# Layer 3 of a four-layer program: another order of three engines' instruction lists

## The chip, the cores and the metric

One core of one Trainium2 chip. A core has TensorE (PE), VectorE (DVE), ScalarE (ACT), GpSimd (POOL) and SyncE (SP, which only issues DMAs here). Each works through its own list of instructions in order, and they wait for each other by semaphores. The metric is the device time of the whole program in microseconds, lower is better; a change under 0.2% can't be told from none.

## What is computed

A residual stream x of 16 batches of 256 tokens, 128 wide, goes through four layers, each of the form below. The change touches layer 3 alone.

```python
xn = _layernorm(x, axis=-1)
x = x + _L3_attn_ref(xn, ...) + _L3_ffn_ref(xn, ...)

# _L3_attn_ref: a state space scan over time, 16 states for each of 128 channels
delta = softplus(x @ W_delta.T);  B = x @ W_B.T;  C = x @ W_C.T;  A = -exp(A_log)
h = h * exp(delta_t * A) + (delta_t * x_t) * B_t;   y_t = sum_n h * C_t
context = (_layer_norm(y) @ W_ctx.T) * context_scale

# _L3_ffn_ref: 8 routed experts (top 2 by router logits, softmax gates) and 2 shared ones
expert(xf) = silu(xf @ w1) * (xf @ w3) @ w2
```

## The kernel before

The program is built by Python generators. A generator holds what one engine does for one batch in one stage, and each `yield` parts it into steps. In layer 3 turn t works on several batches at once: the router and norm of batch t+1 (`pre3`), delta, B and C of batch t (`inner3`), the experts of batch t in two halves of 128 tokens (`moe0`, `moe1`), the scan of batch t-1 (`states3`), and the norm and projection of the scan's result of batch t-2 (`post3`). `turn3` (L2423) hands these six generators of one engine to `merge` (L45), once for each of TensorE, VectorE and ScalarE. A `yield` gives the time in the turn at which the step behind it is due, and `merge` always lets the generator with the smallest due time go on. The times order the list only; the chip waits for semaphores, not for times. GpSimd's list (`po_states3`, L2049) and SyncE's (`sp_layer3`, L2168) are written out directly.

The steps of VectorE, by stage and number, are:
- `states3` (L1194), for each of four groups g of four states: steps 1, 3, 5, 7 are the scan of 128x1024 elements (L1203), steps 2, 4, 6, 8 the product h = dtu * Brep for the next group (L1212; step 8 for group 0 of the next batch). A scan waits for ScalarE's decays dA (L1711) and that product. The product waits for the copy of B to all partitions, which is a DMA of SyncE (L2165), and for TensorE's sum over the group's old contents (L402).
- `inner3` (L1168): 1 copies B and C (L1174) and z (L1177) out of PSUM; 2 is a maximum (L1180); 3 makes delta (L1187) and dtu (L1191).
- `moe` (L1250): 1 clips (L1255); 2 multiplies the projections (L1261, L1262, L1265, L1266, all with a PSUM operand); 3 multiplies by the gates (L1271); 4 adds the second projection (L454 on TensorE) to x (L1275).
- `pre3` (L1122): 1 adds the gathered rows to x (L1128, two of them); 2 and 3 are statistics (L939, L944); 4 normalizes (L957); 5 reads the router's logits and finds the two largest (L1133 to L1143); 6 and 7 make the gates (L1147 to L1165).
- `post3` (L1215): 1 copies the turned sums (L1222); 2 statistics (L1227, L1231); 3 normalizes (L1237); 4 scales (L1243); 5 adds to x (L1247), which releases the store of the batch.

TensorE's: `pre3` 1 turns xn (L370), 2 router (L376); `inner3` 1 B, C (L387) and z (L388); `moe` 1 first projection (L438 to L441), 2 turns hs (L449), 3 second projection (L454); `states3` 1 to 4 sums a group (L402); `post3` 1 turns s (L414), 2 turns st (L419), 3 projects (L424). ScalarE's: `pre3` 1 rstd (L1614, L1616), 2 copies xnT (L1626), 3 the gate's exp (L1694); `inner3` 1 softplus (L1914 to L1918); `moe` 1 two exponentials (L1738, L1740), 2 sigmoid (L1743, L1745), 3 copies hT (L1750, L1751); `states3` 1 to 4 the decays dA of a group (L1711, four each); `post3` 1 copies s (L1722), 2 rstd (L1725, L1727). GpSimd multiplies each group by C behind its scan (L2054) and, behind the second of them, issues two gathers (L2045). TensorE's sum of the group waits for that.

## Time and profile before

| | us |
|---|---|
| median of three runs | 3218.11 (3212.95 to 3218.94) |
| the profiled execution | 3212.44, of it span 3211.1 |
| layer 3, from the end of layer 2's drain | about 2653 to 3211 |
| busy over the whole span: TensorE, VectorE, ScalarE, GpSimd | 2501.2, 2231.2, 1427.3, 835.2 |

Spans count from the first instruction on. A row of a timeline has the start in us, the duration in us, the engine and line, and in brackets the idle time of that engine just ahead and what ended it. A duration contains the time in which a started instruction can't go on, so a long one of an instruction that is otherwise short is itself a reading. Busy time of VectorE contains such times too.

### The profile page before, as it was taken

To read this page: it belongs to the slowest core of one execution; us is meant where nothing else is said; L and a number is where in the kernel's file an instruction comes from. 1 tells how busy PE (TensorE), PEld (TensorE's weight loads), DVE (VectorE), ACT (ScalarE), POOL (GpSimd) and SP (SyncE) were. 2 spreads that over 40 slices of the span, in tenths; PEclk is the share of its full clock that TensorE was granted. 3 is DMA by queue.
4 is the path that set the end of the run, shared out by engine and by line. 5 is a ranking of instruction groups with operands and counts; after the bars stand their busy time and mean duration, and the time that the engine had idled before them with its cause. 6 is when DMAs were issued, how large, how long until landed. Compare 5 with 4: busy or idle time off the path is not lost.

```text
span 3211.1 us, 47743 instructions
## 1 busy us (share of the span) xinstructions
PE 2501.2 (78%) x18201; PEld 1749.2 (54%) x18201; DVE 2231.2 (69%) x4587; ACT 1427.3 (44%) x3688; POOL 835.2 (26%) x453
## 2 busy tenths in 40 slices
PE   4788888888887767888888888867999975677776
PEld 2455555556555654555656556544666663454444
DVE  3488888888887544666576666644666626999997
ACT  0344534544445114565555656532433333444443
POOL 0033343333444301222222222210000002333332
PEclk9899999999999877999999999977999997888887
DMA  1010110110111440000000000000000003444342
GB/s 58 21 34 28 47 35 28 41 41 28 41 41 40 136 168 1 1 1 1 1 1 1 1 1 1 1 32 13 27 27 14 8 25 109 147 128 153 127 152 86
DMA packets 71348, 147.97 MB, mean 46 GB/s; under 512 B 6864, under 2 KB 37072, under 8 KB 70608
## 3 DMA queue, kind: packets, MB, share of 16 engines
q1 hardware_dynamic: 69072, 140.73, 13.3%
q0 software_dynamic: 2048, 4.20, 0.4%
q8 instruction: 144, 2.36, 0.3%
q14 instruction: 84, 0.69, 0.1%
HBM read 135.20 MB, written 9.18 MB: 45 GB/s over the span
## 4 chain that ended last, share of the span: by engine, by line
PE 29%; DVE 16%; issue 13%; ACT 9%; POOL 5%; DMA 2%; SPq 0%; DVEq 0%; POOLq 0%; ACTq 0%
POOL h L2054 4%; ACT pr L1764 3%; PE psum L578 2%; DVE mx L1282 2%; PE psum L325 2%; PE psum L470 2%; PE psum L504 2%; PE psum L515 2%; PE psum L582 2%; PE psum L347 2%; DVE mx L1326 1%; PE psum L774 1%; ACT pt L1808 1%; PE psum L587 1%; POOL got L2045 1%
## 5 line engine op out<-in xcount | busy, mean ns | idle before, releaser
L2020 POOL TENSOR_TENSOR h<-h,Crep 128x1024 f32<-128x1024 f32 x128 | 383.5, 3006 | 700.9 <-DVE h L1444 700.9
L2002 POOL TENSOR_TENSOR pr<-pr,rsum 128x512 f32<-128x512 f32 x192 | 228.0, 1191 | 741.5 <-DVE rsum L1294 741.5
L1326 DVE TENSOR_REDUCE mx<-psum 128x4 f32<-128x1024 f32 (+1 forms) x192 | 228.9, 1216 | 111.8 <-PE psum L587 111.7
L1444 DVE TENSOR_TENSOR_SCAN h<-dA,h 128x1024 f32<-128x1024 f32 x128 | 291.8, 2294 | 2.4 <-ACT dA L1905 1.8
L774 PE MATMUL psum<-h,pack_wf 128*128 128x256 f32 x1024 | 254.3, 405 | 5.4 <-POOL h L2020 5.4
L2054 POOL TENSOR_TENSOR h<-h,Crep 128x1024 f32<-128x1024 f32 x64 | 150.7, 2355 | 346.2 <-DVE h L1203 346.2
L1808 ACT ACTIVATE pt<-psum 128x1024 f32<-128x1024 f32 x192 | 187.5, 1022 | 95.4 <-PE psum L589 95.3
L774 PEld LDWEIGHTS psum<-h,pack_wf 128*128 128x128 f32 x1024 | 206.7, 206 | 42.0 <-POOL h L2020 6.4
L1764 ACT ACTIVATE pr<-psum,nb 128x256 f32<-128x256 f32 (+1 forms) x512 | 211.8, 441 | 31.0 <-DVE nb L1286 31.0
L1905 ACT ACTIVATE dA<-delta,A 128x255 f32<-128x255 f32 x512 | 210.2, 495 | 12.2 <-DVE h L1444 10.8
L1435 DVE TENSOR_TENSOR h<-dtu,psum 128x512 f32<-128x512 f32 x256 | 163.9, 676 | 68.7 <-PE psum L761 61.9
L1774 ACT ACTIVATE prT<-psum 128x512 f32<-128x512 f32 x192 | 114.9, 599 | 183.7 <-PE psum L484 182.9
L402 PE MATMUL psum<-h,pack_wf 128*128 128x256 f32 x512 | 150.1, 444 | 54.0 <-POOL h L2054 53.0
L320 PE MATMUL psum<-xnT,pack_wf 128*128 128x256 f32 x512 | 153.6, 427 | 21.7 <-ACT qT L1667 15.0
L402 PEld LDWEIGHTS psum<-h,pack_wf 128*128 128x128 f32 x512 | 105.7, 217 | 87.3 <-POOL h L2054 72.4
L1294 DVE RECIPROCAL rsum<-sums 128x2 f32<-128x2 f32 (+1 forms) x192 | 31.8, 166 | 168.6 <-ACT pr L1764 166.3
L578 PE MATMUL psum<-kT,qT 32*128 32x128 f32 (+1 forms) x2048 | 119.7, 361 | 37.5 <-ACT pt L1808 29.0
L1203 DVE TENSOR_TENSOR_SCAN h<-dA,h 128x1024 f32<-128x1024 f32 x64 | 146.2, 2284 | 0.3
L582 PE MATMUL psum<-qT,kT 32*128 32x256 f32 (+1 forms) x2048 | 119.9, 363 | 23.5 <-DVE mx L1326 20.8
L2029 POOL DMA_INDIRECT slots<-xn,sloti x32 | 30.9, 966 | 410.3 <-DVE sloti L1119 405.4
L470 PE MATMUL psum<-kT,qT 64*128 64x256 f32 (+1 forms) x1024 | 125.5, 382 | 12.9 <-ACT pr L1764 12.9
L1282 DVE TENSOR_REDUCE mx<-psum 128x2 f32<-128x512 f32 (+1 forms) x192 | 131.5, 685 | 5.5 <-PE psum L474 4.9
(342 smaller groups left out, 5632.8 us busy)
## 6 DMA issues: line engine op xcount, KB each, us to landing
Crep<-c_rows SPq DMA_DIRECT2D x64, 512.0 KB, 3.8
Brep<-bc_rows SPq DMA_DIRECT2D x64, 512.0 KB, 6.5
Crep<-bc_rows SPq DMA_DIRECT2D x64, 512.0 KB, 5.7
w1r<-m_w SPq DMA_DIRECT2D x32, 256.0 KB, 5.6
w2r<-m_w SPq DMA_DIRECT2D x32, 256.0 KB, 5.4
pack_wf<-wf SPq DMA_DIRECT2D x1, 3192.0 KB, 13.4
slots<-zero SPq DMA_DIRECT2D x12, 256.0 KB, 3.0
w1s<-s_w SPq DMA_DIRECT2D x8, 256.0 KB, 2.8
```

What stands on the lines that cost most here:

```text
L402: i = pe.e.matmul(bk, k.w["ident"], k.h[g][:, n, :], start=g == 0 and n == 0, stop=g == 3 and n == NG - 1)
L470: pe.e.matmul(k.bank[r][:, n * wid:(n + 1) * wid], qT[rows, g, q * P:(q + 1) * P], kT[rows, g, 0:wid], start=n == 0, stop=True, skip_group ...
L774: i = pe.e.matmul(YB[:, c * L:(c + 1) * L], w["ident"], h[:, n, :], start=g == 0 and n == 0 and c == 0, stop=g == 3 and n == NG - 1, skip_ ...
L1282: ve.e.tensor_reduce(mx[:, 0:nh], k.bank[r][:, :].rearrange("p (h k) -> p h k", h=nh), AX.X, ALU.max).then_inc(*ve.step())
L1326: ve.e.tensor_reduce(mx[:, qb, 2 * h:2 * h + 2, groups[0]:groups[-1] + 1], k.psum[:, base:base + 2, :].rearrange("p i (n x) -> p i n x", n ...
L1444: ve.e.tensor_tensor_scan(flat(h), flat(k.dA[c][g % 2]), flat(h), 0.0, ALU.mult, ALU.add).then_inc(*k.set("scanned", 0, b, g, c))
L1764: i = ac.e.activation(pr[:, h * wid:(h + 1) * wid], bk[:, h * wid:(h + 1) * wid], ACT.Exp, bias=nb[:, h:h + 1], scale=float(HD[1]) ** -0.5 ...
L1808: ac.e.activation(k.pt[2 * c + h][:, :], k.psum[:, base:base + 2, :].rearrange("p i x -> p (i x)"), ACT.Exp, scale=float(HD[l]) ** -0.5).t ...
L1905: i = ac.e.activation(k.dA[c][g % 2][:, n, 1:], k.delta[x % 2][:, c, 1:], ACT.Exp, scale=k.A0[:, c, g * NG + n:g * NG + n + 1])
L2002: po.e.tensor_tensor(p3, p3, bcast(k.rsum[n][:, 0:len(heads[r])], P * (q + 1), 2), ALU.mult).then_inc(*k.set("normed", 1, b, p, r))
L2020: po.e.tensor_tensor(h[:, :, :], h[:, :, :], k.Crep[n % 3][:, :, :], ALU.mult).then_inc(*k.set("hC", 0, b, g, c))
L2054: po.e.tensor_tensor(k.h[g][:, :, :], k.h[g][:, :, :], k.Crep[g][:, :, :], ALU.mult).then_inc(*k.set("hC", 3, b, g))
```

## The change

`merge` takes an explicit table in place of due times: for each engine and stage the places of its steps. The stage with the smallest place goes on, and the first place of each tuple is that of what stands ahead of the first `yield`, which issues nothing. All `yield` values are dropped, and so are the constants that fed them (`STATES_AT`, `EXPERTS_AT`, `TURN` and others). For layers 0, 1 and 2 the table has places of its own as well; only layer 3's part is shown.

```diff
-def merge(*stages):
+def merge(order, *stages):
     live = []
-    for n, stage in enumerate(stages):
-        if stage is not None:
-            gen, first, last, steps = stage
-            live.append([first, n, gen, first, (last - first) / steps])
+    for n, (gen, name) in enumerate(x for x in stages if x is not None):
+        live.append([n, gen, iter(order[name])])
+    live = [[next(at), n, gen, at] for n, gen, at in live]
     while live:
-        now = min(live, key=lambda x: (x[0], x[1]))
-        slot = next(now[2], None)
-        if slot is None:
+        now = min(live, key=lambda x: x[:2])
+        if next(now[2], run) is run:
             live.remove(now)
         else:
-            now[0] = now[3] + slot * now[4]
+            now[0] = max(now[0], next(now[3]))
...
-TURN = {0: 57, 2: 24, 3: 37}
-STATES_AT, EXPERTS_AT = (0, 9, 18, 27), (0, 13.4)
+ORDER = {
...
+    3: {
+        "pe_inner3": (2, 8),
+        "pe_moe0": (3, 6, 11, 12),
+        "pe_moe1": (4, 9, 17, 18),
+        "pe_post3": (0, 7, 13, 19),
+        "pe_pre3": (5, 10, 15),
+        "pe_states3": (1, 14, 16, 20, 21),
+        "ve_inner3": (3, 13, 18, 28),
+        "ve_moe0": (4, 5, 11, 16, 27),
+        "ve_moe1": (6, 19, 23, 26, 35),
+        "ve_post3": (0, 10, 17, 22, 30, 34),
+        "ve_pre3": (7, 8, 12, 15, 20, 31, 33, 36),
+        "ve_states3": (1, 2, 9, 14, 21, 24, 25, 29, 32),
+        "ac_inner3": (2, 18),
+        "ac_moe0": (3, 8, 9, 16),
+        "ac_moe1": (4, 12, 15, 19),
+        "ac_post3": (0, 7, 14),
+        "ac_pre3": (5, 13, 17, 20),
+        "ac_states3": (1, 6, 10, 11, 21),
+    },
+}
```

Written out by steps (stage.number), a full turn of layer 3 is, before and after:

```
VectorE before: states.1 inner.1 post.1 states.2 inner.2 post.2 inner.3 moe0.1 post.3
  states.3 post.4 moe0.2 states.4 moe0.3 pre.1 pre.2 pre.3 moe1.1
  states.5 moe0.4 moe1.2 post.5 states.6 moe1.3 pre.4
  states.7 moe1.4 pre.5 states.8 pre.6 pre.7
VectorE after:  states.1 moe0.1 pre.1 states.2 post.1 moe0.2 pre.2 inner.1
  states.3 pre.3 moe0.3 post.2 inner.2 moe1.1 pre.4 states.4 post.3 moe1.2
  states.5 states.6 moe1.3 moe0.4 inner.3
  states.7 post.4 pre.5 states.8 pre.6 post.5 moe1.4 pre.7
TensorE before: inner.1 post.1 moe0.1 states.1 post.2 post.3 moe1.1 moe0.2 states.2
  moe0.3 states.3 moe1.2 pre.1 moe1.3 pre.2 states.4
TensorE after:  moe0.1 post.1 inner.1 moe1.1 pre.1 moe0.2 moe0.3 post.2 states.1
  pre.2 states.2 moe1.2 moe1.3 post.3 states.3 states.4
ScalarE before: post.1 moe0.1 inner.1 states.1 post.2 moe0.2 states.2 moe1.1 moe0.3
  pre.1 moe1.2 states.3 moe1.3 pre.2 states.4 pre.3
ScalarE after:  states.1 post.1 moe0.1 moe0.2 states.2 states.3 moe1.1 pre.1 post.2
  moe1.2 moe0.3 pre.2 inner.1 moe1.3 pre.3 states.4
```

## Rows read from the trace of the kernel before

**Rows 1.** The page: busy tenths of VectorE in 40 slices of the span.
```profile
DVE  3488888888887544666576666644666626999997
```
**Rows 2.** Windows: busy us and instructions of each engine, granted clock, DMA.
```profile
2852.91:2884.79 31.88, 22.83 (x95) 15.96 (x95) 29.55 (x62) 15.25 (x38) 12.17 (x6) 0.82 0.45 141
```
**Rows 3.** Timeline: the first scan, and the one that opens the last turn.
```profile
2692.03 2.28 DVE L1203 TENSOR_TENSOR_SCAN h<-dA,h 128x1024 f32<-128x1024 f32 x1
...
3175.33 2.29 DVE L1203 TENSOR_TENSOR_SCAN h<-dA,h 128x1024 f32<-128x1024 f32 x1
```
**Rows 4.** Groups of VectorE, 2800 to 3000: busy us, mean ns, idle ahead.
```profile
L1255 DVE TENSOR_SCALAR he<-he 128x640 f32<-128x640 f32 x13 | 6.4, 491 | 2.5 <-ACT he L1740 2.5
...
L1275 DVE TENSOR_TENSOR X<-X,psum 128x128 f32<-128x128 f32 x12 | 3.5, 288 | 11.9 <-PE psum L454 11.9
```
**Rows 5.** Timeline of the turn: a scan, GpSimd's products and VectorE's steps beside them.
```profile
2852.91 2.28 DVE L1203 TENSOR_TENSOR_SCAN h<-dA,h 128x1024 f32<-128x1024 f32 x1
...
2855.28 2.36 POOL L2054 TENSOR_TENSOR h<-h,Crep 128x1024 f32<-128x1024 f32 x1 [4.90 <-DVE h L1203]
...
2856.20 2.52 DVE L1212 TENSOR_TENSOR h<-dtu,Brep 128x1024 f32<-128x1024 f32 x1
...
2863.40 0.52 DVE L1243 TENSOR_SCALAR lT<-psum,pack_wf 128x256 f32<-128x256 f32 x1
...
2863.84 0.68 DVE L1261 TENSOR_TENSOR hs<-he,psum 128x512 f32<-128x512 f32 x1
...
2868.69 0.25 DVE L944 BATCH_NORM_AGGREGATE mv<-stats 128x2 f32<-128x6 f32 x2
...
2879.90 2.34 POOL L2054 TENSOR_TENSOR h<-h,Crep 128x1024 f32<-128x1024 f32 x1 [5.49 <-DVE h L1203]
...
2880.54 0.17 DVE L1133 TENSOR_TENSOR lg<-psum,pack_wf 128x16 f32<-128x16 f32 x1
...
2881.32 0.95 DVE L1143 TENSOR_TENSOR g<-m 128x2 f32<-128x2 f32 x1
```
**Rows 6.** Lines: ns minimum, median, maximum of one instruction; first and last start.
```profile
L1212 DVE TENSOR_TENSOR h<-dtu,Brep x64: 1210/1450/3273, 2689.4 to 3191.3; 128x1024 f32<-128x1024 f32 x64
...
L1143 DVE TENSOR_TENSOR g<-m x16: 143/944/948, 2663.3 to 3140.7; 128x2 f32<-128x2 f32 x16
...
L1128 DVE SCALAR_TENSOR_TENSOR X<-got,scl,X x32: 339/340/353, 2657.5 to 3127.2; 128x128 f32<-128x128 f32 x32
...
L1271 DVE TENSOR_TENSOR hs<-hs,gt x32: 677/682/693, 2674.1 to 3168.8; 128x512 f32<-128x512 f32 x32
```
**Rows 7.** Other layers: timeline of layer 0 and of layer 1, then a group.
```profile
1039.58 0.67 DVE L1420 TENSOR_TENSOR delta<-zab,zmx 128x512 f32<-128x512 f32 x1
1039.74 2.72 POOL L2020 TENSOR_TENSOR h<-h,Crep 128x1024 f32<-128x1024 f32 x1 [5.95 <-DVE h L1444]
1040.28 2.73 DVE L1424 TENSOR_TENSOR dtu<-delta,su 128x512 f32<-128x512 f32 x1
...
1727.53 1.11 DVE L1523 SCALAR_TENSOR_TENSOR f<-f,f 128x704 f32<-128x704 f32 x1
...
1728.72 0.85 DVE L1523 SCALAR_TENSOR_TENSOR f<-f,f 128x704 f32<-128x704 f32 x1
...
L1535 DVE TENSOR_TENSOR f<-f,f4s 128x704 f32<-128x704 f32 x16 | 25.8, 1611 | 0.6
```
**Rows 8.** Timeline of turn 0: VectorE's waits.
```profile
2681.09 0.29 DVE L1275 TENSOR_TENSOR X<-X,psum 128x128 f32<-128x128 f32 x1 [2.84 <-PE psum L454]
...
2688.24 0.29 DVE L1275 TENSOR_TENSOR X<-X,psum 128x128 f32<-128x128 f32 x1 [3.73 <-PE psum L454]
```
**Rows 9.** The copies of B (L2165), issue to landing; four of ScalarE's decays, timeline.
```profile
DMA to landing us min/median/max: 3.5/6.5/8.8
...
2858.46 1.69 ACT L1711 ACTIVATE dA<-delta,A 128x255 f32<-128x255 f32 x4
```
**Rows 10.** Window of 2 us, columns as in rows 2.
```profile
2862.00:2864.00 2.00, 0.02 (x1) 0.03 (x1) 2.00 (x3) 1.90 (x5) 0.43 (x1) 0.50 0.98 379
```

More of the change, by code:

```diff
@@ L202 @@
 OPENS = {1: 0, 2: 1, 4: 3}
-STEP1, TURN1, PROJ1 = 8, 48, 8.8
-QKV1, V1 = tuple(2.2 + 4.2 * j for j in range(8)), (35, 38, 41, 44.5)
-GATE1, HQ1 = (14.3, 20.6), (42.2, 42.9, 43.9)
 GROUPS = {0: 4, 1: 8, 2: 4}
@@ L681, in pe_wide @@
             if (half, i) in ((0, 3), (1, 5)):
[L682 removed]
+                yield
                 pe_pv(k, l, b, half)
[L684 removed]
+    yield
     if b + 1 < NB:
@@ L779, in pe_states @@
 def pe_states(k, b):
-    for at, g, j in SPREADS_AT:
-        yield at
+    for g, j in SPREADS:
+        yield
         if g is None and 0 <= b + j // 4 < NB:
@@ L962, in ve_pre0 @@
     ve, bk, w = k.ve, k.bank[PRE_BANK[0]], k.w
-    yield from ve_norm(k, 0, b, 11.3, 4.6)
-    yield 24.6
+    yield from ve_norm(k, 0, b)
+    yield
     ve.wait_ge(*k.at("gate", b))
@@ L1073, in ve_pre2 @@
     i.then_inc(*ve.step())
-    yield from done_at(14)
+    yield from rest()
     for q in range(QT):
@@ L1129, in ve_pre3 @@
     i.then_inc(*k.set("x_gathered", b))
-    yield from ve_norm(k, 3, b, 16, 8.5)
-    yield 30
+    yield from ve_norm(k, 3, b)
+    yield
     ve.wait_ge(*k.at("router", b))
@@ L1345, in ve_wide0, with ve_out @@
 def ve_wide0(k, l, b):
-    for c, h, at in MAXIMA_AT:
-        yield at
-        if b + 1 < NB:
-            ve_max(k, 0, b + 1, c, h)
-def ve_out(k, l, b, at):
+    for c in range(3):
+        for h in range(2):
+            yield
+            if b + 1 < NB:
+                ve_max(k, 0, b + 1, c, h)
+def ve_out(k, l, b):
     ve, w, bk = k.ve, k.w, k.bank[OUT_BANK[l]]
@@ L1447, in ve_states @@
 def ve_states(k, b):
-    steps = [(SCANS_AT[g][c], g, c, True) for g in range(4) for c in range(CI)]
-    steps += [(at, g, j, False) for at, g, j in PRODUCTS_AT]
-    for at, g, n, scan in sorted(steps):
-        yield at
-        if scan and 0 <= b < NB:
-            ve_scan(k, b, g, n)
-        if not scan and 0 <= b + g // 4 < NB:
-            ve_product(k, b + g // 4, g % 4, n)
+    for g in range(4):
+        yield
+        if 0 <= b < NB:
+            ve_scan(k, b, g, 0)
+        yield
+        if 0 <= b < NB:
+            ve_scan(k, b, g, 1)
+        for j in range(2):
+            yield
+            if 0 <= b + (g + 1) // 4 < NB:
+                ve_product(k, b + (g + 1) // 4, (g + 1) % 4, j)
 def ve_results(k, b):
     ve, w, YB, su = k.ve, k.w, k.bank[Y_BANK], k.su[b % 2]
-    yield 10.8
+    yield
     ve.wait_ge(*k.at("summed", 0, b, 3, 1))
@@ L1494, in ve_experts0, with ve_fp4 @@
             ve.e.tensor_tensor(k.oall[:, :, e], k.bank[2 + e % 2][:, 0:NB], bcast(w["m_b2"][:, e], NB, 1), ALU.add).then_inc(*k.set("oall", e))
-def ve_fp4(k, name, b, out, src, nblk, at, pace=1):
+def ve_fp4(k, name, b, out, src, nblk):
     ve = k.ve
@@ L1581, in ve_ffn @@
     ve.wait_ge(*k.at("hh", b, 1))
-    yield from ve_fp4(k, "h", b, blocks(k.hq[:, :, :]), blocks(k.hh[:, :, :]), QT * NBH, 26.3, 1.4)
-    yield 47
+    yield from ve_fp4(k, "h", b, blocks(k.hq[:, :, :]), blocks(k.hh[:, :, :]), QT * NBH)
+    yield
     ve.wait_ge(*k.at("down1", b))
@@ L1672, in ac_pre2 @@
     ac, bk, w = k.ac, k.bank[PRE_BANK[2]], k.w
-    yield from ac_norm(k, 2, b, 0, 4)
-    yield 8.5
+    yield from ac_norm(k, 2, b)
+    yield
     ac.wait_ge(*k.at("gate_in", 2, b))
@@ L1690, in ac_pre3 @@
     ac = k.ac
-    yield from ac_norm(k, 3, b, 16.6, 9)
-    yield 33
+    yield from ac_norm(k, 3, b)
+    yield
     ac.wait_ge(*k.at("gate_in", 3, b))
@@ L1697, in ac_inner3 @@
 def ac_inner3(k, b):
-    yield from ac_softplus(k, 3, b, 1, 3.4)
+    yield from ac_softplus(k, 3, b, 1)
 def ac_states3(k, b):
     ac = k.ac
-    for at, x, g in ((5, b, 1), (13, b, 2), (21.5, b, 3), (30, b + 1, 0)):
-        yield at
+    for x, g in ((b, 1), (b, 2), (b, 3), (b + 1, 0)):
+        yield
         if not 0 <= x < NB:
@@ L1888, in ac_inner @@
     ac.e.activation(k.sig[:, :, :], k.sig[:, :, :], ACT.Exp, scale=-1.0).then_inc(*k.set("sig", "z", b))
-    yield from ac_softplus(k, 0, b, CI, 42.3)
+    yield from ac_softplus(k, 0, b, CI)
 def ac_states(k, b):
     ac = k.ac
-    for at0, at1, n in DECAYS_AT:
+    for n in range(1, 5):
         x, g = b + n // 4, n % 4
@@ L2380, in layer1, with turn2 @@
         phase_end(k, q, "layer1")
-def turn2(k, t, pre, wide, out):
-    T = TURN[2]
-    merge((pre(k, t + 2), 0, T, T) if t + 2 < NB else None,
-          (out(k, 2, t - 1, OUT_AT[2]), 0, T, T) if out is not None and t else None,
-          (wide(k, 2, t), 0, T, T) if wide is not None and t < NB else None)
+def turn2(k, t, e, pre, wide, out):
+    merge(ORDER[2],
+          (pre(k, t + 2), e + "_pre2") if t + 2 < NB else None,
+          (out(k, 2, t - 1), e + "_out") if t else None,
+          (wide(k, 2, t), e + "_wide") if t < NB else None)
 def layer2(k, t2, t3):
```

467 lines of the change are left out of this document (249 added, 218 removed).

## The prediction, blind

> **What bounds the kernel now.** I read the page first: by slices of the span of 3211.1 us, VectorE is at nine tenths or more in the last ones alone [rows 1]. Those slices are layer 3, the only layer whose lists the change reorders. The windows cut it by turns: from the scan at 2852.91 to the one at 2884.79 a turn takes 31.88 us, and VectorE is busy for 29.55 of them, TensorE for 22.83 at a granted clock of 0.82, ScalarE for 15.25, GpSimd for 12.17 [rows 2]. So VectorE's list sets the turn. The fifteen turns between the first scan at 2692.03 and the last turn's at 3175.33 take 483.3 us, 32.22 each [rows 3]; a turn 0 without scans stands before them, a tail of 35.8 us behind.
>
> Next I asked what VectorE's turn holds besides its own work, because a reordering can only change that. There are two things.
> - It idles for 11.9 us in 200 ahead of the expert additions (L1275, behind the second projection) and for 2.5 ahead of L1255 [rows 4]. By turns of 31.88 that is 2.3 us each.
> - It is **held by GpSimd**. The product h*dtu (L1212) takes 1.21 us when GpSimd is quiet [rows 6], but 2.52 at 2856.20, where GpSimd's own product (L2054, 2.36 us, to 2857.64) is still running, and it ends 1.1 us behind that. The median of its 64 is 1.45, which is the case of the second group, where some 0.2 us is held. A subtraction of two columns (L1143) takes 0.95 us at 2881.32 and ends with GpSimd's at 2882.24; its quickest is 0.14 [rows 5, 6]. Together 1.3 + 0.2 + 0.8 = 2.3 us a turn.
>
> The bare list is then 31.9 - 2.3 - 2.3 = 27.3 us. I take 27.5, since small waits between steps that depend on each other stay in any order.
>
> **What the change does to it, part by part.** I walked both merges. In layers 0 to 2 each engine's list comes out in the order that it has now, so this costs nothing, on nothing's cover: no instruction moves. In layer 3 every instruction of a turn is still issued once a turn; nothing is added, and no DMA or wait of SyncE or GpSimd changes place. Only what stands behind what on three engines is new.
>
> (a) *The waits on TensorE.* L1275 of the first half moves from directly behind the third scan to behind L1212 and a product of the gates. The second half's goes almost to the end of the turn, and TensorE's sums (L402) move behind the projections. The second projection's results are then there well before VectorE asks, and L1255 stands behind a 2.28 us scan, where ScalarE has caught up. That takes 2.3 us a turn away. What is late next? TensorE gets its xn, hs and lT in the order in which VectorE now makes them, so its gaps grow but nobody on VectorE waits for it. I leave 0.3 us for new waits.
>
> (b) *What stands behind each scan.* This is the term that I expect to decide. GpSimd's product starts 0.09 us behind a scan's end (2855.19 to 2855.28) and lasts 2.36 [rows 5]. In the old order mostly steps with a PSUM input stand there, and these are not held (L1243 and L1261, right behind the second scan, 0.52 and 0.68 us) [rows 5]. What happens to others is seen in other layers [rows 7]. L1420, two SBUF inputs, starts at 1039.58 ahead of GpSimd's 1039.74: it runs its 0.67 us, GpSimd's product is stretched to 2.72, and the next two-input step, L1424, takes 2.73 at the same size. So who starts first goes first, and a waiting GpSimd gets its turn between two back-to-back steps of VectorE. In layer 1, where GpSimd's products are shorter, L1523 (scalar_tensor_tensor, the kind of L1128) takes 1.11 instead of 0.85, and L1535, whose second operand is broadcast like L1271's, 1.61 in the mean of sixteen at that same width. Along the new VectorE list:
> - First scan. L1255 (0.49 us [rows 4]) starts first, then GpSimd takes 2.36, and L1128, moved there with two SBUF inputs, is held for all of it: 2.4 us. Now 1.3 is lost there.
> - Second scan. Only L944 (0.25 for both [rows 5]) stands ahead of L1271, hs by a broadcast gate. Held until 0.09 + 2.36 behind the scan: 2.2 us. Now 0.2.
> - Third scan. L1212 comes directly behind it and is first; GpSimd follows, and L1271 behind L1212 is held for 2.36 us. Now none.
> - Fourth scan. L1243, L1133, L1137 and L1141 (0.44 from L1243's start to the next, 0.78 from L1133's start to L1143's [rows 5]) are not held; L1143 is, for 2.45 - 1.22 = 1.2 us. Now 0.8.
>
> Sum: 2.4 + 2.2 + 2.4 + 1.2 = 8.2 us held in place of 2.3. No row of this trace has L1128 or L1271 beside GpSimd's product. The lower bound of their price is zero (L1128 always takes 0.34, L1271 0.68 [rows 6], but GpSimd's product never ran beside them; a gain is excluded, since company makes no step shorter). The upper is GpSimd's whole 2.36. I take the upper, by the nearest rows (L1424, L1523, L1535: same kinds of operands), and keep zero as a rival.
>
> The Trainium skill ("SBUF — State Buffer", the section on SBUF's two separate sides) calls this an exclusive lock: of GpSimd's op and a VectorE op with two SBUF inputs or in a 2-port mode, the first gets the port pair for the whole instruction and the other fully blocks. By that rule L1128 and L1271 are held in full and the turn is the 36.0 us below; by the lines that rows name alone it would be rival 1's 30.4. The trace agrees for L1212 and L1424, and shows nothing of the two.
>
> (c) *Per turn*: 27.5 + 8.2 + 0.3 = **36.0 us**, against 32.22: +3.8, times fifteen = +57.
>
> (d) *Turn 0 and the tail.* Turn 0 has no scans, so nothing is held and the waits decide: 2.84 us and 3.73 ahead of L1275 [rows 8]. The moved additions lose 6.6 of these; about 1.4 comes back, because TensorE transposes the first half's hs only behind the next batch's xn, and L1261 of the second half needs that buffer: -5, and -6 with smaller ones (0 at the least, if as much comes back elsewhere). In the tail two of three products L1212 (held up to 3.27 us [rows 6]) stand directly behind a scan and run first, which gives back 2 us each on VectorE, but GpSimd's products start 1.2 us later for it and they feed the last sums: -2.
>
> (e) *The DMAs.* SyncE's list keeps its order but follows VectorE: the row store that waits for L1174 goes out 7 us later in the turn (behind L939, just ahead of the second scan, where now it is directly behind the first). The copy of B that L1212 needs behind the third scan is queued after it as the third of five. Landing takes 6.5 us in the median and at most 8.8 [rows 9]. In the new turn the store goes some 10 us in and the copy at 12.5; it lands by 19 to 21 and is wanted at 22 to 23: hidden, with 1 us of cover in the worst case. The copies for the second and third products have 10 us. On ScalarE the softplus moves far back, but delta is wanted only behind the third scan; the last decay of the turn (L1711, 1.7 us for the four [rows 9]) is queued behind the gate's exp, which waits for L1143. L1143 + 0.2 + 1.7 us ends 1 to 1.5 us before the next scan: L1212 (1.2) and a dozen small steps cover it.
>
> **Sum.** The profiled execution took 3212.44 us, 3211.1 of it span: 3212.4 + 57 - 6 - 2 = 3261. It lies 5.7 under the median of the three runs (3218.11, from 3212.95), which a profile alone can't explain; on the median's footing it is 3267. I predict 3263, between the two and towards the profiled one.
>
> **The rivals.**
> 1. *The hold doesn't reach the moved steps* (faster). If L1128 and L1271 run beside GpSimd at no price, the turn holds L1212 behind the first scan for 2.45 - 0.41 - 0.64 = 1.4 and L1143 for 1.2: 27.5 + 2.6 + 0.3 = 30.4, or some 31.2 with waits that the holds had covered (TensorE's second projection behind its later transposes). Fifteen turns give -15, or -27 by 30.4, and with -8 the time is 3185 to 3195. For it: no row has them together. Against it: L1535 and L1523. It decides if either kind is free. Chance 0.07.
> 2. *Half a hold* (a little slower or the same). If VectorE keeps its right of way through back-to-back steps, the first scan costs nothing, and GpSimd comes in behind L1271 after the third, to hold L1187 instead for about 2.2: 27.5 + 0.3 + 2.2 + 2.2 + 1.2 = 33.4 a turn, 3212 + 18 - 8 = 3222. L1424 speaks against it. Chance 0.09, of which 0.04 within 0.2%.
> 3. *TensorE becomes the bound too* (slower still). Its list now has gaps of 6 us while VectorE is held (from L388 to the second half's projection, which waits for L1266). From 2862 to 2864, where TensorE waits for L1243's result and is busy for 0.02 of 2 us, the granted clock is 0.50 (1.2 GHz) [rows 10]. At 0.5 throughout, its 22.83 us at 0.82 become 37.4, and a turn 37.5 to 38.5: 3212 + 80 to 94 - 8 = 3284 to 3299. It needs the low clock everywhere, where the old turn had it in a third. A late B copy, 1 to 2 us a turn, would give 3276 to 3291. Chance 0.12 for both.
> 4. *The order isn't new* (only the notation changes): the walk excludes it.
>
> **How the numbers follow.** My forecast has 0.72. Its own range is 3243 to 3278: a per-turn error of 1 us makes 15. The range that should hold 8 in 10 reaches down to rival 2 and up into rival 3: 3222 to 3286; rival 1, half of rival 2 and the upper third of rival 3 lie outside. A change under 0.2% (6.4 us) can't be told from none here. Faster 0.07, within 0.04, slower 0.89.
>
> **What would show it.** In the changed profile: L1271 with a median near 3.0 us instead of 0.68 and L1128's first of two near 2.7; L1212 behind the third scan at 1.2, and GpSimd's product there 3.3 to 3.5 us long; no idle time ahead of L1275; turns of 36 us with VectorE busy for over 95%. I am wrong if L1271 and L1128 keep 0.68 and 0.34, if VectorE waits on ScalarE's dA or on B copies, or if TensorE has no idle time left.

## The result and the profile after

The changed kernel is slightly slower, where I had forecast clearly slower.

| | before | after |
|---|---|---|
| median of nine runs each | 3218.94 us (3212.95 to 3225.28) | 3227.06 us (3222.07 to 3238.30) |
| ratio to before, 95% interval | | 1.0030 [1.0019, 1.0042] |
| predicted | | 3263 (3222 to 3286) |
| the profiled execution, of it span | 3212.44, 3211.1 | 3238.30, 3237.0 |

So some 10 us were lost, not 44. (One execution of a kernel below, of 3482 us with a granted clock of 0.71 where its others have 0.89, is left out of its median and ratio.) The profiled execution of the changed kernel is the longest of its nine, so its total can't be set against the other's. Layers 0 to 2 have the same instructions in the same order on every engine, yet layer 3 begins (first ScalarE step on its own weights) 2652.85 us into the span before and 2669.07 after. In all kernels below, which share this code, it begins between 2644.39 and 2669.07. Stages of layer 3 repeat far better: the kernel before and the one below that has its order in the full turns take 32.22 and 32.26 us a turn, the changed kernel and one that only moves a step from hold to hold take 33.75 each, and turn 0 takes 28.4 to 30.9 in the nine kernels that have it in the changed order (or with one step moved). So every account here starts at that step. "Turn" is the distance between the first scans of two batches, the mean of fifteen. "Turn 0" is what stands before the first of them, "tail" what stands behind the last full turn.

```
                 layer 3   turn 0   turn, mean of 15   tail
before             558.2     39.2        32.22         35.8
after              567.9     29.4        33.75         32.3
after - before      +9.7     -9.8      15 x +1.53      -3.5
forecast             +49       -6      15 x +3.8         -2
```

The 9.7 us of layer 3 are 0.0030 of the whole, which is the measured ratio. The signs of all three terms are those forecast. The forecast of the turn is too large by 2.25 us, fifteen times.

After the change a full turn from the middle looks like this as a window (span, then busy us of TensorE, its weight loads, VectorE, ScalarE and GpSimd, granted clock, DMA share, GB/s), the counterpart of [rows 2]:

```profile
2866.70:2900.94 34.24, 25.09 (x103) 18.40 (x102) 33.52 (x63) 15.35 (x40) 13.62 (x6) 0.75 0.36 132
```

VectorE is busy for 33.5 of 34.2 us, 98%, where before it was 29.55 of 31.88. Its groups between 2800 and 3000 (busy us, mean ns, then idle ahead) show what the busy time consists of. L1317, L1175, L1227, L1190, L1259, L1301, L1307 and L1321 are before's L1271, L1128, L1180, L1143, L1212, L1255, L1261 and L1275:

```profile
L1259 DVE TENSOR_TENSOR h<-dtu,Brep 128x1024 f32<-128x1024 f32 x23 | 27.8, 1208 | 0.0
L1317 DVE TENSOR_TENSOR hs<-hs,gt 128x512 f32<-128x512 f32 x12 | 20.9, 1740 | 0.0
L1175 DVE SCALAR_TENSOR_TENSOR X<-got,scl,X 128x128 f32<-128x128 f32 x12 | 16.2, 1391 | 0.0
L1227 DVE TENSOR_SCALAR zmx<-zin 128x256 f32<-128x256 f32 x6 | 10.6, 1758 | 0.0
L1307 DVE TENSOR_TENSOR hs<-he,psum 128x512 f32<-128x512 f32 x12 | 8.1, 676 | 1.3 <-PE psum L507 1.3
L1190 DVE TENSOR_TENSOR g<-m 128x2 f32<-128x2 f32 x6 | 8.0, 1333 | 0.0
...
L1321 DVE TENSOR_TENSOR X<-X,psum 128x128 f32<-128x128 f32 x11 | 3.0, 277 | 0.0
```

The additions (L1321) wait for nothing, against 11.9 us before, and the product h (L1259) takes its quiet 1.21 [rows 4, 6]. In their place four other lines are long: L1317 is 1.74 in the mean, L1175 1.39, L1227 1.76, L1190 1.33, although no operand has changed. The timeline of the turn tells who is long beside whom:

```profile
2868.99 0.49 DVE L1301 TENSOR_SCALAR he<-he 128x640 f32<-128x640 f32 x1
2869.39 2.71 DVE L1175 SCALAR_TENSOR_TENSOR X<-got,scl,X 128x128 f32<-128x128 f32 x2
...
2878.59 0.65 DVE L1317 TENSOR_TENSOR hs<-hs,gt 128x512 f32<-128x512 f32 x1
2879.17 0.47 DVE L1274 BATCH_NORM_STATS2 stats<-st 128x6 f32<-128x128 f32 x2
2879.67 0.25 DVE L1278 BATCH_NORM_AGGREGATE mv<-stats 128x2 f32<-128x6 f32 x2
2879.84 1.76 DVE L1227 TENSOR_SCALAR zmx<-zin 128x256 f32<-128x256 f32 x1
...
2888.42 1.20 DVE L1259 TENSOR_TENSOR h<-dtu,Brep 128x1024 f32<-128x1024 f32 x1
2889.53 2.83 DVE L1317 TENSOR_TENSOR hs<-hs,gt 128x512 f32<-128x512 f32 x1
...
2896.67 1.33 DVE L1190 TENSOR_TENSOR g<-m 128x2 f32<-128x2 f32 x1
```

and GpSimd's products by C in the same turn, one for each scan:

```profile
2869.06 2.63 POOL L2103 TENSOR_TENSOR h<-h,Crep 128x1024 f32<-128x1024 f32 x1 [5.31 <-DVE h L1250]
2878.61 2.84 POOL L2103 TENSOR_TENSOR h<-h,Crep 128x1024 f32<-128x1024 f32 x1 [6.91 <-DVE h L1250]
...
2888.58 3.23 POOL L2103 TENSOR_TENSOR h<-h,Crep 128x1024 f32<-128x1024 f32 x1 [4.12 <-DVE h L1250]
2895.64 2.35 POOL L2103 TENSOR_TENSOR h<-h,Crep 128x1024 f32<-128x1024 f32 x1 [3.82 <-DVE h L1250]
```

Every long step of VectorE ends within 0.6 us behind a product of GpSimd. Behind the first scan the clip (L1301) starts 0.07 us ahead of GpSimd and runs in its 0.49, and then L1175 is held: 2.71 for two that take 0.60 undisturbed in the kernel before, so 2.1 us. Behind the second scan the multiplication by the gates (L1317) starts 0.02 us ahead of GpSimd and escapes. Two statistics run unhindered, and the maximum of z (L1227) is held, 1.76 against 0.28: 1.5 us. Behind the third, L1259 is first, GpSimd's product is stretched to 3.23, and L1317 takes 2.83 against 0.68: 2.15 us. Behind the fourth, L1190 loses 1.33 - 0.14 = 1.2 us. The sum is 6.9 us a turn. The rest, 34.2 - 6.9 - 0.3 of waits, is 27.0 us of VectorE's own work.

### The profile page after: what moved, and what is told of

Read it like the earlier page. It is cut to its first block, busy times and chain, and to the rows that moved or that the text cites. A ratio compares the mean times of both kernels' runs of the same rounds, so it can differ in the third digit from the quotient of the medians.

```text
span 3237.0 us, 47770 instructions
## 1 busy us (share of the span) xinstructions
PE 2532.7 (78%) x18201; PEld 1784.4 (55%) x18201; DVE 2288.6 (71%) x4587; ACT 1425.6 (44%) x3688; POOL 858.1 (27%) x453
## 3 DMA queue, kind: packets, MB, share of 16 engines
q8 instruction: 144, 2.36, 0.3%
## 4 chain that ended last, share of the span: by engine, by line
PE 40%; DVE 36%; ACT 11%; issue 7%; DMA 2%; POOL 0%; DVEq 0%; SPq 0%; ACTq 0%
PE psum L821 4%; DVE h L1250 4%; DVE h L1493 4%; PE psum L637 3%; ACT pr L1814 3%; DVE mx L1374 3%; PE psum L641 3%; DVE h L1484 3%; PE psum L384 2%; PE psum L528 2%; PE psum L646 2%; DVE h L1259 2%; DVE mx L1328 2%; PE psum L573 2%; PE psum L770 2%
## 5 line engine op out<-in xcount | busy, mean ns | idle before, releaser
L2069 POOL TENSOR_TENSOR h<-h,Crep 128x1024 f32<-128x1024 f32 x128 | 383.3, 3004 | 709.3 <-DVE h L1493 709.3
L2103 POOL TENSOR_TENSOR h<-h,Crep 128x1024 f32<-128x1024 f32 x64 | 175.9, 2748 | 333.6 <-DVE h L1250 333.6
L821 PEld LDWEIGHTS psum<-h,pack_wf 128*128 128x128 f32 x1024 | 212.6, 212 | 44.4 <-POOL h L2069 6.0
L1340 DVE RECIPROCAL rsum<-sums 128x2 f32<-128x2 f32 (+1 forms) x192 | 31.9, 166 | 168.1 <-ACT pr L1814 165.9
L641 PE MATMUL psum<-qT,kT 32*128 32x256 f32 (+1 forms) x2048 | 128.1, 380 | 20.1 <-DVE mx L1374 17.4
L2078 POOL DMA_INDIRECT slots<-xn,sloti x32 | 30.9, 964 | 419.8 <-DVE sloti L1166 414.9
L302 PE MATMUL psum<-mask,identb 128*128 128x512 bf16 x496 | 125.6, 385 | 8.4 <-DVE qT L1032 7.9
```

What stands on the lines that cost most here:

```text
L641: pe.e.matmul(banks[r][:, cols], kT[row:row + 32, kg, k0:k0 + P], qT[row:row + 32, g, k0:L], start=n == 0, stop=True, skip_group_check=True)
L821: i = pe.e.matmul(YB[:, c * L:(c + 1) * L], w["ident"], h[:, n, :], start=g == 0 and n == 0 and c == 0, stop=g == 3 and n == NG - 1, skip_ ...
L2069: po.e.tensor_tensor(h[:, :, :], h[:, :, :], k.Crep[n % 3][:, :, :], ALU.mult).then_inc(*k.set("hC", 0, b, g, c))
```

## The experiments

In the diffs a list is written by steps, as in the section on the change; unnamed lists are as they were. A ratio is that of a kernel's executions to those of the kernel before on the same chip, with its 95% interval; the microseconds beside it are the kernel's median, which isn't the same from chip to chip.

### Is it GpSimd's product that makes those steps long?

The product by C is cut to 8 of its 1024 columns, once in the old order and once in the new; the sums over the states are then of unmultiplied values. Nothing else changes, and all waits stay.

```diff
-po.e.tensor_tensor(k.h[g][:, :, :], k.h[g][:, :, :], k.Crep[g][:, :, :], ALU.mult)...
+po.e.tensor_tensor(k.h[g][:, :, 0:2], k.h[g][:, :, 0:2], k.Crep[g][:, :, 0:2], ALU.mult)...
```

> The order of before, with GpSimd's product of layer 3 (h*Crep, 128x1024, 2.36 us) cut to 8 of its 1024 columns, so that it can hardly hold VectorE; the product by C is left out of the result for the rest. Theory (VectorE's list sets the turn, and what the orders differ by is how long GpSimd holds it): in the trace of before the held times are 2.3 us a turn, so this kernel gains 30 to 40 us: 3179 to 3189. Rival (the orders differ by waits on TensorE or ScalarE or by TensorE's clock, GpSimd's hold is small for both): the same gain within 10 us in this kernel and in its twin with the new order, below.

> The same cut in the changed kernel. Theory: its trace shows 6.9 us held a turn (L1128's first 2.1, the maximum of z 1.5, L1271's second 2.2, L1143 1.2), so it gains up to 15 x 6.9 = 104 us, less what new waits on TensorE take back: I expect 80 to 100, 3127 to 3147, which makes the new order 35 to 60 us faster than the old one once GpSimd is quiet. Rival: it stays 5 to 15 us behind its twin, at about 3190 to 3200.

Measured: 0.9908 [0.9879, 0.9937], 3181.0 us, in the old order, and 0.9742 [0.9714, 0.9769], 3124.5 us, in the new. Both were as the theory of the hold had it; the second is 2.5 us under its expected times. The groups of VectorE of the new order with the short product, 2800 to 3000:

```profile
L1317 DVE TENSOR_TENSOR hs<-hs,gt 128x512 f32<-128x512 f32 x14 | 9.4, 671 | 0.0
L1301 DVE TENSOR_SCALAR he<-he 128x640 f32<-128x640 f32 x14 | 6.9, 491 | 7.8 <-ACT he L1790 7.8
...
L1175 DVE SCALAR_TENSOR_TENSOR X<-got,scl,X 128x128 f32<-128x128 f32 x14 | 4.3, 346 | 0.0
...
L1227 DVE TENSOR_SCALAR zmx<-zin 128x256 f32<-128x256 f32 x7 | 1.8, 261 | 0.0
...
L1190 DVE TENSOR_TENSOR g<-m 128x2 f32<-128x2 f32 x7 | 1.0, 143 | 0.0
```

All four steps are back at their short times. VectorE now waits 7.8 us in 200 for ScalarE instead, which the holds had covered. The turn is 27.81 us, and in the old order 30.91. The holds account for the new order's gain: a turn of 34.1 us, less 7.0 of holds and 0.3 of waits, plus the 1.3 of waits that VectorE has now, makes 28.1. So without GpSimd in the way the new order is 1.7% **better** than the old one (0.9742 against 0.9908). The full product costs the new order 2.9% (from 0.9742 to 1.0030), the old one 0.9%.

### How much is turn 0 alone?

The old order everywhere, but turn 0 in the new one.

```diff
-merge(order of the kernel before) in all turns of layer 3
+merge(changed order) for t == 0, order of the kernel before for t > 0
```

> The order of before in all turns of layer 3 but turn 0, which has the new one. Theory: turn 0 has no scans and so no hold; in the traces it takes 38.8 us before and 29.0 after, and this kernel keeps those 9.8 us: 3209, ratio 0.997. Rival (the wait is only passed on to turn 1, which must then wait for sums, copies or decays that come no earlier): 3218, ratio 1.000.

Measured: 0.9963 [0.9944, 0.9982], 3194.94 us. By the account, turn 0 takes 28.5 us against 39.2, the turns 32.26 against 32.22, the tail 35.7 against 35.8. So the gain is 10.7 us in turn 0 and 10.1 in the whole layer: it is separate from the rest, and only 0.6 comes back in the fifteen turns. The waits that I had costed, 2.84 and 3.73 ahead of the additions [rows 8], were not all. Turn 0 of the kernel before has eight waits of over a microsecond on VectorE, 21.7 us together, that of the changed kernel six of 12.2 us. Among the eight is this one for the softplus, which the new turn 0 does without:

```profile
2669.44 0.43 DVE L1187 TENSOR_TENSOR delta<-zab,zmx 128x256 f32<-128x256 f32 x1 [3.28 <-ACT zab L1918]
```

### Does a single moved wait bring anything?

The old order, with the addition of the first half (moe0.4, the step with most of the 11.9 us) moved behind the next multiplication and the addition of the norm's projection. It is one part of what the change does, done by itself.

```diff
 VectorE
-states.5 moe0.4 moe1.2 post.5 states.6 moe1.3
+states.5 moe1.2 post.5 moe0.4 states.6 moe1.3
```

> The order of before with one step moved on VectorE: the first half's addition L1275 goes from directly behind the third scan to behind the second half's products and the addition of post3. This is the part of the change that takes a wait on TensorE away, alone. Theory: in the trace both additions wait 2.0 us a turn, the first for about two thirds of it, so 0.7 to 1.2 us a turn, 10 to 18 us in all, ratio 0.995 to 0.997. Rival (the wait only goes to L1261 or the transposes, which need what stands behind it): 1.000.

Measured: 0.9995 [0.9986, 1.0004], 3219.11 us: nothing, where I had expected 0.3 to 0.5%. Waits of VectorE, 2800 to 3000 (line, waited for, us in total, times, longest), before and then here:

```profile
DVE X L1275 <- PE psum L454: 11.9, 12, 2.2
DVE he L1255 <- ACT he L1740: 2.5, 7, 0.4
```

```profile
DVE hs L1307 <- ACT he L1795: 9.6, 6, 2.1
DVE X L1321 <- PE psum L512: 2.3, 6, 0.4
DVE he L1301 <- issue: 1.8, 5, 0.4
DVE he L1301 <- ACT he L1790: 0.4, 1, 0.4
```

The wait for TensorE has gone from 11.9 to 2.3 us, but the step that takes its place (L1307, the second half's multiplication) now asks ScalarE for the sigmoid 1.6 us a turn too early. The sum is 14.1 after 14.4. So this step by itself doesn't collect the gain, since the next one waits for ScalarE, which stands in the same chain. The new order shifts the lists of all three engines, and there the additions wait for nothing; with the short product this is worth 3.1 us a turn (27.81 against 30.91). No other single move was tried against these waits.

### Can one step be moved out of a hold?

The changed kernel, with VectorE's second scan moved ahead of the first half's multiplications (moe0.2), which then stand behind it. The steps of moe0.2 read PSUM, and should run beside GpSimd's second product unheld.

```diff
 VectorE
-post.1 moe0.2 pre.2 inner.1 states.3 pre.3 moe0.3
+post.1 states.3 moe0.2 pre.2 inner.1 pre.3 moe0.3
```

> The changed kernel with one step moved on VectorE: the second scan stands in front of the products with PSUM operands (L1261 to L1266 of before) instead of behind them and what follows. Theory (a hold is what is left of GpSimd's 2.36 us once the steps that it doesn't hold have run behind the scan): some 2.9 us of such steps now stand there, so the 1.5 us held behind this scan go to zero: 15 x 1.5 = 22 us faster than the changed kernel, ratio to before 0.996. Rival (VectorE is full either way and the hold only moves to another step): ratio 1.003, as the changed kernel.

Measured: 1.0019 [1.0010, 1.0028], 3229.57 us, turn 33.56. Missed: no more than a tenth of a per cent better than the changed kernel. The second scan's hold is gone as expected, but this came up in its place:

```profile
2892.81 2.28 DVE L1250 TENSOR_TENSOR_SCAN h<-dA,h 128x1024 f32<-128x1024 f32 x1
...
2896.36 1.51 DVE L1301 TENSOR_SCALAR he<-he 128x640 f32<-128x640 f32 x1 [1.27 <-ACT he L1790]
```

```profile
2895.17 2.35 POOL L2103 TENSOR_TENSOR h<-h,Crep 128x1024 f32<-128x1024 f32 x1 [5.31 <-DVE h L1250]
```

The clip behind the first scan has to wait 1.27 us for ScalarE, so GpSimd (2895.17) is there first and holds it for another 1.0. In the changed kernel the clip had started first, by 0.07 us in the turn above. Over 200 us VectorE waits 9.1 for ScalarE ahead of L1301 and 2.5 for B copies.

The other edit of this kind leaves the second scan and moves the second half's multiplications (moe1.2) from ahead of the third scan to behind its product h:

```diff
 VectorE
-states.4 post.3 moe1.2 states.5 states.6 moe1.3
+states.4 post.3 states.5 states.6 moe1.2 moe1.3
```

> The changed kernel with one other step moved on VectorE: the second half's products with PSUM operands (1.7 us) go from in front of the third scan to behind L1212, which follows that scan. Theory: GpSimd starts when L1212 ends, 1.7 of its 2.36 us lie beside steps that it doesn't hold, and the L1271 behind them is held for 0.7 instead of 2.15 us: 15 x 1.45 = 22 us faster than the changed kernel, ratio to before 0.996. Rival (these products then make the transposes and the second projection late, and VectorE waits for TensorE instead): ratio 1.000 or above.

Measured: 0.9947 [0.9933, 0.9960], 3207.98 us, turn 32.06: as expected, and a little better, since 0.33 us of the hold are left where I had expected 0.7. In this row L1317 behind the third scan, formerly 2.83, takes 1.01, since 1.83 us of PSUM steps run beside GpSimd's product first:

```profile
2908.51 1.01 DVE L1317 TENSOR_TENSOR hs<-hs,gt 128x512 f32<-128x512 f32 x1
```

So a change that was slower becomes faster than both by moving one step of one list.

### Who is held: does the order of starts decide?

The changed kernel's L1317 behind the second scan escaped by 0.02 us. Two steps are exchanged, so that the statistics come first.

```diff
 VectorE
-states.3 pre.3 moe0.3 post.2 inner.2
+states.3 pre.3 post.2 moe0.3 inner.2
```

> The changed kernel with one pair of VectorE's steps exchanged: behind the second scan it goes on with pre.3, post.2 (statistics, 2 x 0.24 and 0.2), moe0.3 instead of pre.3, moe0.3, post.2. In the changed kernel moe0.3's multiplication by the gates starts 0.02 us ahead of GpSimd's product (2878.59 against 2878.61) and runs unheld in 0.65; the next locking operation, the maximum of z, is held and lasts 1.76 instead of 0.28. My theory is that this start order alone decides who is held and for how much. Here post.2 stands in between, so GpSimd's product starts first and runs its 2.36 from about 0.16 behind the scan: the multiplication by the gates should be held (about 2.2 in place of 0.68, so 1.5) and the maximum of z not (0.3). What is hidden behind the product is then 0.8 of unlocked work instead of 0.8 plus the 0.6 of the multiplication that had got through ahead, but GpSimd's product also starts 0.6 sooner, so the sum of both effects is between 0 and +0.6 a turn, 0 to +9 us over 15 turns: ratio against the kernel before 1.003 to 1.006, likeliest 1.003. Rival: start order does not decide, and the multiplication by the gates goes ahead all the same (0.68) with the maximum of z at 1.7: ratio 1.003 too, but its rows tell it.

Measured: 1.0035 [1.0022, 1.0049], 3231.97 us, a full turn 34.22. Now GpSimd's product (2871.09, 2.34) is first:

```profile
2871.71 2.26 DVE L1317 TENSOR_TENSOR hs<-hs,gt 128x512 f32<-128x512 f32 x1
2873.90 0.28 DVE L1227 TENSOR_SCALAR zmx<-zin 128x256 f32<-128x256 f32 x1
```

The roles are exchanged, 2.26 and 0.28 instead of 0.65 and 1.76, and the time is the same, because in both orders the same 0.7 us of statistics run beside GpSimd. Two more kernels ask whether VectorE can keep GpSimd out by a run of back-to-back instructions, as it seemed to do once in the changed kernel's first full turn: there L1317, L1227 and L1301 ran in 0.65, 0.27 and 0.47, GpSimd's product took 3.45, and L1004 behind them was held.

```diff
 VectorE, maximum behind the product h
-pre.3 moe0.3 post.2 inner.2 moe1.1 ... states.5 states.6 moe1.3
+pre.3 moe0.3 post.2 moe1.1 ... states.5 states.6 inner.2 moe1.3
 VectorE, maximum behind the gates
-pre.3 moe0.3 post.2 inner.2 moe1.1
+pre.3 moe0.3 inner.2 post.2 moe1.1
```

> The changed kernel with the maximum of z (inner.2) moved from the second scan's to the third scan's followers: product h, maximum of z, multiplication by the gates. In the changed kernel's first full turn the maximum ran right behind the multiplication by the gates in 0.27, and GpSimd's product, asked for since 2709.89, got in only behind the clip after it and lasted 3.45. So VectorE kept the ports through three back-to-back instructions there; behind the product h, where the multiplication by the gates follows, it did not. Theory K: an instruction with an immediate scalar and one input, back to back behind a locking one, keeps the ports. Then the maximum takes 0.28 here, GpSimd's product behind the third scan is 3.4 to 3.5 long and the multiplication by the gates behind is held for 2.1 (2.8). Theory G: GpSimd gets its turn behind the product h whatever follows. Then the maximum is held (2.4), the multiplication takes 0.68, and GpSimd's product 3.24. Behind the second scan the clip (moe1.1) is the next locking instruction and takes 0.48 plus 1.5 by either. The time is the changed kernel's, 1.003, by either.

> The changed kernel with the maximum of z (inner.2) put directly behind the multiplication by the gates in the second scan's followers, ahead of the statistics (post.2), so that every full turn has the sequence that the first one had. Theory K (an immediate-scalar instruction back to back keeps the ports): the maximum takes 0.27 to 0.28 in all turns, GpSimd's product behind the second scan 3.0 to 3.1 instead of 2.84, and the clip behind the statistics is held for about 1.7 (2.1 to 2.2). Theory G (GpSimd gets its turn behind each instruction, and the first turn was an accident of hundredths): the maximum is held for its whole, 2.3 to 2.4, and the clip takes 0.48, as the statistics then hide nothing: turn +0.7. Ratio 1.003 to 1.004 by K, 1.006 by G.

Measured: 1.0035 [1.0023, 1.0046], 3230.73 us, and 1.0060 [1.0041, 1.0080], 3236.56 us, late full turns 34.1 and 34.76. Behind the product, and then behind the gates:

```profile
2738.10 1.20 DVE L1259 TENSOR_TENSOR h<-dtu,Brep 128x1024 f32<-128x1024 f32 x1
2739.21 2.44 DVE L1227 TENSOR_SCALAR zmx<-zin 128x256 f32<-128x256 f32 x1
2741.57 0.68 DVE L1317 TENSOR_TENSOR hs<-hs,gt 128x512 f32<-128x512 f32 x1
```

```profile
2766.23 0.65 DVE L1317 TENSOR_TENSOR hs<-hs,gt 128x512 f32<-128x512 f32 x1
2766.81 2.42 DVE L1227 TENSOR_SCALAR zmx<-zin 128x256 f32<-128x256 f32 x1
```

Theory G in both: GpSimd gets in behind the first instruction, whatever comes next, and the next locking one (one of those that GpSimd's product can hold) is held for all of 2.15 us (2.42 - 0.27), which the statistics, now behind it, no longer shorten. That costs 0.6 us a turn, and it is in the time, with 1.0060. Why three instructions got through in the first full turn stays open: GpSimd started 0.01 us behind L1317 there (2709.89 after 2709.88), and just so in the row above, where it got in. It is one turn of fifteen, but hardly chance: in the first full turn of three other kernels (products_third, race_lost and max_behind_gates) GpSimd's product behind the second scan takes 3.45 as well, and L1317 and L1227 run unheld. So "GpSimd gets in behind the first instruction" is the rule of the fourteen later turns, not of all.

### Can the rule be turned into a faster order?

With the durations of the traces and one rule (behind a scan, a VectorE step of SBUF operands alone is held until GpSimd's product is through, a step with PSUM is not, and neither are the statistics) I walked many orders of all three lists and took the shortest.

```diff
 VectorE
-states.1 moe0.1 pre.1 states.2 post.1 moe0.2 pre.2 inner.1 states.3 pre.3 moe0.3 ...
+pre.1 states.1 states.2 post.1 post.2 inner.1 pre.2 post.3 moe0.1
+states.3 inner.2 pre.3 moe0.2 post.4 inner.3 states.4 moe0.3 pre.4 moe1.1
+states.5 states.6 moe1.2 pre.5 states.7 moe1.3 moe0.4 post.5 pre.6 states.8 pre.7 moe1.4
 TensorE
+inner.1 post.1 moe0.1 post.2 states.1 moe1.1 post.3 moe0.2 pre.1 states.2 pre.2
+moe0.3 states.3 moe1.2 moe1.3 states.4
 ScalarE
+post.1 states.1 post.2 moe0.1 moe0.2 inner.1 pre.1 states.2 moe1.1 moe1.2 states.3
+pre.2 moe0.3 states.4 pre.3 moe1.3
```

> An order of all three lists of layer 3 of my own, put together so that steps which GpSimd doesn't hold stand behind each scan and no step of VectorE waits for TensorE. Walked through with the durations of the trace, with the port pair going to whoever starts first, VectorE's turn comes to 28.5 to 29 us, against 32.2 before and 33.75 after the change: 15 x 3.4 = 51 us less, and some 8 in turn 0 and the tail: 59 us faster than before, ratio 0.981. If the theory of the hold is wrong in its size or order rule, the turn stays above 31 and the ratio above 0.99.

Measured: 0.9796 [0.9782, 0.9809], 3155.12 us; turn 0 33.9, turn 28.33 in the mean, tail 32.4. Its followers of a scan show why:

```profile
2870.50 2.27 DVE L1250 TENSOR_TENSOR_SCAN h<-dA,h 128x1024 f32<-128x1024 f32 x1
2872.70 0.25 DVE L1227 TENSOR_SCALAR zmx<-zin 128x256 f32<-128x256 f32 x1
2872.88 0.23 DVE L991 BATCH_NORM_AGGREGATE mv<-stats 128x2 f32<-128x6 f32 x2
2873.04 0.64 DVE L1307 TENSOR_TENSOR hs<-he,psum 128x512 f32<-128x512 f32 x1
2873.61 0.27 DVE L1308 TENSOR_TENSOR hs<-he,psum 128x128 f32<-128x128 f32 x1
2873.91 0.69 DVE L1311 TENSOR_TENSOR hs<-hs,psum 128x512 f32<-128x512 f32 x1
2874.52 0.28 DVE L1312 TENSOR_TENSOR hs<-hs,psum 128x128 f32<-128x128 f32 x1
```

```profile
2872.85 2.36 POOL L2103 TENSOR_TENSOR h<-h,Crep 128x1024 f32<-128x1024 f32 x1 [3.14 <-DVE h L1250]
```

The maximum of z slips in ahead of GpSimd, and the PSUM multiplications run beside its product, in their normal times. Of the four steps that were long in the changed kernel none is here (L1317 0.68, L1175 0.35, L1227 0.26 and L1190 0.14 in the mean). One long step is left, a copy of 16 columns that turns integers into floats, from SBUF to SBUF, behind the fourth scan:

```profile
L1194 DVE CAST rf<-i 128x16 f32<-128x16 uint32 x7 | 12.6, 1793 | 0.0
```

Its turn 0 is longer than that of the changed kernel, so I took both:

```diff
-merge(the order above) in all turns of layer 3
+merge(changed order) for t == 0, the order above for t > 0
```

> My own order of the three lists with turn 0 in the changed kernel's order. In the run of my own order alone layer 3 took 491.3: turn 0 33.9, 15 turns of 28.33, tail 32.4; in the changed kernel turn 0 took 29.4 and in the kernel before with its turn 0 28.5. If turn 0 is a stretch by itself, as the run of turn 0 alone said, this saves 4.5 to 5.4 us more: ratio against the kernel before 0.978, where the own order gave 0.9796. Rival: what turn 0 saves, the first full turns give back, since the lists behind it wait for steps that it has put off (the delta of batch 0 late in its list): ratio 0.9796.

Measured: 0.9776 [0.9763, 0.9788], 3149.76 us, turn 0 28.9, turn 28.37, tail 33.8. Of the 5.0 us that turn 0 saves, the tail returned 1.4 and the fifteen turns 0.6. The two intervals overlap, so it is the account (layer 3 in 488.3 us against 491.3) that speaks for the second. It is the fastest of the kernels that compute everything, 2.2% under the kernel before.

## Why the prediction was too high

The mechanism was the right one and decided the sign; no rival took its place. The step that failed is the sizing of the turn, (b) and (c): I priced the four holds at 8.2 us a turn, where 6.95 were measured, took 27.5 us for VectorE's own work, where it was 27.0, and counted a middle turn of 36.0 fifteen times, where the mean is 0.45 under a middle turn. That made +57 us of what were +23. In (d) I was too low by 5.3 us of gain.

| term of the sum | predicted | measured |
|---|---|---|
| waits of VectorE left per full turn (a) | 0.3 | 0.34 |
| held behind the first scan (b) | 2.4 | 2.1 |
| second | 2.2 | 1.5 |
| third | 2.4 | 2.15 |
| fourth | 1.2 | 1.2 |
| VectorE's own work per turn | 27.5 | 27.0 |
| full turn (c) | 36.0 | 34.2 |
| mean of the fifteen | 36.0 | 33.75 |
| turn 0, tail (d) | -6, -2 | -9.8, -3.5 |

- **(a)** held. The waits ahead of the additions are gone and what is new comes to 0.34 us, ahead of L1307.
- **(b), the price of a full hold.** I took GpSimd's whole 2.36 us for a step right behind. Measured is 2.10 (L1175), 2.15 (L1317), 2.15 (L1227 behind the gates). A held instruction shows 0.2 us less than GpSimd's duration. Over the first and the third scan that makes 0.55 us a turn.
- **(b), the second scan.** Here I had L1317 held with only 0.14 us in front of it. It started 0.02 us before GpSimd instead, so its own 0.6 us ran unheld, and the two statistics, which are not held by anything, then ran beside GpSimd's product. That 0.7 us difference is the largest single error. Winning the start counts only by what it puts ahead of the held step. With GpSimd first and the statistics ahead of L1317, the turn was the same; with L1317 first and L1227 right behind it, the hold was the full 2.15. My walk had stopped at the first locking step.
- **Own work.** 27.5 was 27.3 rounded up for small gaps; measured 27.0. The 27.3 itself took the mean wait (2.3 us) off the turn of 31.88, which has only 1.8 of waits (the old turns alternate between 31.9 and 33.0, and the longer wait is in the longer ones). By that turn's own waits it is 27.7. So the new order's own work is 0.7 us shorter than the old. No step is shorter by more than a few hundredths; the gaps from one start to the next are, where the next step needs the result of the one before. The aggregate L944 starts 0.52 us behind L939 (2868.17 and 2868.69), while in the new order a copy starts 0.39 behind the same statistics (2875.21 and 2875.60); behind L1154 0.19 become 0.08, and with the gaps around L944 and the additions this comes to 0.66. I had written that such small waits stay in any order: they don't.
- **(c), the ends.** I multiplied the full turn by fifteen. The first has no norm of an earlier batch (33.35 us), and the last no next batch (30.83). The last saves that by less work and not by shorter holds: the product h behind its first scan takes 3.38 us in L1175's place. Four more, the second to the fifth, take 33.7 to 33.8, because VectorE has no wait for TensorE (L1307) in them. In these four the granted clock is 0.80. From the sixth on it is 0.75, and there the wait of 0.34 us comes up: a turn with it takes 34.1, the sixth 34.24. Here are the fourth turn's window and the wait in the sixth:

```profile
2799.32:2833.01 33.69, 23.63 (x98) 17.10 (x97) 33.31 (x63) 15.13 (x40) 13.49 (x6) 0.80 0.39 134
...
2884.49 0.69 DVE L1307 TENSOR_TENSOR hs<-he,psum 128x512 f32<-128x512 f32 x1 [0.34 <-PE psum L507]
```

The mean is 0.45 under the turn of 34.2: 7 us in all. Together, 1.3 for the holds, 0.5 for the own work and 0.45 for the ends make the 2.25 us a turn that the forecast was too high.
- **(d)** Turn 0 alone gives 10.7 us by its account, not 6: with it goes the wait of 3.28 us for the softplus, that I had not costed. The tail came as described, with L1259 first and GpSimd second, though there the scan itself is then held, which I had not foreseen (below).
- **(e)** held: in the fifteen turns VectorE never waits for a copy of B or for a decay. The copies landed in 3.6 us at the least, 4.1 in the median and 10.1 at most, so the worst case was 1.3 us worse than the 8.8 that I had reckoned with.
- **Rival 1**, that the moved steps are not held, and **rival 2**, that VectorE keeps its right of way through back-to-back steps, are refuted by the rows of L1175 and of L1317 behind L1259. The sum with rival 2's price came nearest to the time (3222), which is luck: it left out the hold of L1175 and put the third one on L1187, and its turn of 33.4, 0.35 too short, cancels against turn 0 and the tail, which it had 5.3 us too long. Rival 1's sum was wrong as well: from 3212 its two turns give 3189 and 3177, where I had written 3185 to 3195. **Rival 3**: the clock did fall, 0.75 against 0.82 in the turn, with TensorE busy for 25.1 of 34.2 us, but VectorE waits for it no more than 0.34 us in each of the turns from the sixth on, and not at all in the four before them at 0.80. So the lower clock goes with some 0.4 us a turn, 4 us in all, as long as VectorE's list is the bound. The two go together in other kernels as well (max_behind_product has 0.80 once more in its tenth turn, without the wait and in 33.71 us, between turns of 34.4 and 34.3 at 0.75), but no run changes the clock alone.

The Trainium skill ("SBUF — State Buffer", the section on SBUF's two separate sides) says that of GpSimd's operation and a VectorE operation with two SBUF inputs or in a 2-port mode the first gets the pair and the other fully blocks. The trace agrees for L1175 and L1317 (2.71 and 2.83 us), but for the 0.2 us by which the holds fall short of GpSimd's duration. It fits the rows of L1227 and L1194 too, which have one input and are held (1.76 and 1.79), if they count as the second kind; I had not put these on my list of locking steps beside the two-input ones.

My range reached from 3222 to 3286 and holds the 3227 measured, close to its lower end. That is luck in part: the reason was not in it, since I had bounded the hold of one step and not what the steps ahead of it hide.

## What to carry to other kernels

In this kernel, with VectorE's list as the bound and GpSimd working out of SBUF beside it, the order within VectorE's list decides how much of GpSimd's work VectorE pays for. In one like it, put steps with a PSUM operand and statistics for the length of GpSimd's instruction behind the step that releases it, and steps with SBUF operands alone elsewhere. Price a hold as GpSimd's duration, here less 0.2 us, less all unlocked work that stands ahead of the next locking step, not by the first locking step alone, and price the first and last turns on their own. And where engines work in a chain, look what the next step will wait for before you count the wait that the profile shows as gain: moving the one addition brought nothing here.
